# Softmax stage of a graph network: the destinations' one-hot made in 16 bits, two tiles innermost, and widened to fp32 by ScalarE

## The chip, the cores and the metric

The kernel runs on one core of a Trainium2 chip. The metric is the device time of one execution in microseconds; lower is better. A time of a kernel is the median of its runs.

## The reference, cut to what matters

Four graph layers run in a row on 3125 nodes with 16 features and 100000 edges sorted by destination. The change is in the second layer, an attention over the edges that end in one node:

```
w_m = (efeat @ W_msg + b_msg).reshape(E, 16, 16)
w_a = (efeat @ W_attn + b_attn).reshape(E, 16, 16)
h_src = feat[src][:, :, None]
e1 = w_m * h_src
e2 = w_a * h_src
seg_max = segment_max(e2, dst)
ex = exp(e2 - seg_max[dst])
denom = segment_sum(ex, dst)
ft = segment_sum(e1 * ex / denom[dst], dst)
out = ft.sum(axis=1)
```

The softmax stage, `soft_sums`, computes `ex` and `e1 * ex` of every edge (256 values each) and sums both by destination. The division by `denom` is left to the stage behind it, `attend`.

## The kernel before

**Tiles.** The edges lie in NT = 832 tiles of 128 slots, an edge to a partition. A block is 128 nodes (NB = 25 blocks), each tile has the edges of one block only, and two neighbouring tiles always share one. The number of a destination within its block is the field `LO` of `m.fields`, which is fp32; holes have -1 there.

**Rounds.** `soft_sums` goes through 416 rounds `r` of two tiles, written out without a loop. Two rounds make a group `n` of four tiles (HB = 4, 208 groups). One round does this:

- TensorE, `network`: four bf16 matmuls of 256 columns give `net_a` and `net_m` in PSUM (three sets of buffers).
- VectorE, `enter`: two operations multiply them by the source's features `m.held`.
- TensorE, `top`: six bf16 matmuls subtract the maxima of the block, which a second one-hot, `hot_t`, spreads over the edges. VectorE makes `hot_t` once per group in `far_hot`.
- ScalarE: `Exp` of `net_a` into `both[..., 0, :]`.
- VectorE, `weigh`: `both[..., 1, :] = net_m * both[..., 0, :]`.
- TensorE, `spread`: for each of the two tiles an fp32 matmul of 512 columns with the one-hot `hot` as weights, into `sums`. The profile has two rows for one such matmul.
- VectorE, `add`: adds `sums` to the row of the block in `m.acc`.

`hot` is the one-hot that this change is about: for each edge 128 fp32 values, 1.0 in the column of its destination. `spread_hot(n)` makes it for four tiles at once with `one_hot` (line 1271): `LO`, repeated over 128 columns, is compared with `m.iota_row`. Both inputs are fp32 in SBUF. It has two buffers, used in turn.

**Order.** Each engine's order is written out by hand. TensorE goes, for round r, `network(r + 3)`, `top(r + 2)`, `spread(r + 1)`. VectorE's order is:

```
for r in range(turns):
    if r % 2 == 0 and r + 2 < turns:
        far_hot(r // 2 + 1)
    if r + 2 < turns:
        enter(r + 2)
    if r + 1 < turns:
        weigh(r + 1)
    add(r)
    if r % 2 == 0 and r + 2 < turns:
        spread_hot(r // 2 + 1)
```

**GpSimd.** Beside this, GpSimd writes the edges' second records into DRAM in another order (`m.slots2`), for a later stage: 832 indirect DMAs, two to a round (line 1533), whose indices `row2` and data `rec2` lie in SBUF. No engine of this stage waits for them. To spread them over the stage, their first in a round waits until `add(r - 2)` is done (`kept`), the second until `weigh(r)` is done (`both_s`). After the last of them GpSimd waits for the landing of all. The stage is a block: `attend`, which begins on VectorE at line 1674, starts when all engines have left it.

**Start.** VectorE's first instruction in the stage is the clearing of `m.acc` (line 1577), then `far_hot(0)`, `spread_hot(0)`, `enter(0)`, `enter(1)`, `weigh(0)`.

Of the kernel before, what the change touches and what calls it, by code (L numbers as in the profile page):

```python
# [5 lines left out]
ALU = mybir.AluOpType  # L6
# [4 lines left out]
BF16 = mybir.dt.bfloat16  # L11
FP16 = mybir.dt.float16

P = 128
# [9 lines left out]
NT = -(-2 * ((E + NB * (2 * P - 1)) // (2 * P)) // (2 * TB)) * 2 * TB  # L24
# [7 lines left out]
WGT, SRC, TIX, LO, SRCC, KEY, LOE, NF = range(8)  # L32
# [24 lines left out]
def makers(nc, ctx, stage):  # L57

    def sb(name, shape, dt=F32):
        return ctx.enter_context(nc.sbuf_tensor(f"{stage}_{name}", shape, dt))  # L60

    def ps(name, shape, dt=F32):
        return ctx.enter_context(nc.psum_tensor(f"{stage}_{name}", shape, dt))

    def sem(name):
        made = nc.alloc_semaphore(f"{stage}_{name}")
        ctx.callback(PAST.append, made)
        return made

    return sb, ps, sem  # L70
# [738 lines left out]
def slot_field(m, t0, n, k):  # L809

    return m.fields[:, bass.ds(t0, n), k]


def blocks_of(nc, m, engine, pair, n):

    _, values = nc.values_load_multi_w_load_instructions(m.pair[0:1, bass.ds(pair, n)], engines=[engine], min_val=0, max_val=NB - 1,
                                                         skip_runtime_bounds_check_because=COUNTED)
    return values
# [412 lines left out]
HB = 4  # L1231
# [38 lines left out]
def one_hot(nc, m, field, n, out):  # L1270
    return nc.vector.tensor_tensor(out, slot_field(m, n * HB, HB, field)[:, :, None].to_broadcast([P, HB, P]),
                                   m.iota_row[:, None, :].to_broadcast([P, HB, P]), ALU.is_equal)
# [218 lines left out]
def soft_sums(nc, m):  # L1491

    turns, sets = NT // 2, 3
    with ExitStack() as ctx:
        sb, ps, sem = makers(nc, ctx, "sm")
        feat, low = sb("feat", [KP, 2, 512], BF16), sb("low", [P, 2, 512], FP16)
        hot_t, hot = sb("hot_t", [P, 2, 512], BF16), sb("hot", [P, 2, HB, P])
        both = sb("both", [P, 2, 2, 2, 256])
        rec2, row2 = sb("rec2", [P, NT, 2]), sb("row2", [P, NT], I32)
        net_a, net_m = ([ps(f"{n}{k}", [P, 2, 256]) for k in range(sets)] for n in ("net_a", "net_m"))  # L1500
        sums = [ps(f"sums{k}", [P, 512]) for k in range(2)]
        loaded = [sem("loaded0"), sem("loaded1")]
        names = ("hot_t_s", "hot_s", "net_s", "arg_s", "mess_s", "tops_s", "exp_s", "both_s", "sums_s", "kept", "cleared",
                 "ordered", "order_in")
        (hot_t_s, hot_s, net_s, arg_s, mess_s, tops_s, exp_s, both_s, sums_s, kept, cleared, ordered,
         order_in) = map(sem, names)
        block = ctx.enter_context(nc.Block())

        @block.sync
        def _(sp):  # L1510
            low_rows = m.low_row.rearrange("(c n) -> c n", n=512)
            feats = m.feat_t.rearrange("k (c n) -> k c n", n=512)
            for n in range(HT):
                h = n % 2
                if n >= 2:
                    sp.wait_ge(net_s, 2 * n - 2)
                    sp.wait_ge(hot_t_s, n - 1)
                sp.dma_start(low[:, h], low_rows[n:n + 1].to_broadcast([P, 512])).then_inc(loaded[h], 16)
                sp.dma_start(feat[:, h], feats[:, n, :]).then_inc(loaded[h], 16)
                if n == 1:  # L1520
                    sp.dma_start(rec2[:, :, :], m.rec2_dram).then_inc(order_in, 16)
                    sp.dma_start(row2[:, :], m.row2_dram).then_inc(order_in, 16)
# [14 lines left out]
        def four(ap):  # L1537
            return ap.rearrange("q t (i o) -> q t i o", o=D)

        @block.vector  # L1540
        def _(dve):
            def far_hot(n):
                h = n % 2
                dve.wait_ge(loaded[h], (n // 2 + 1) * 32)
                if n >= 2:
                    dve.wait_ge(tops_s, 2 * n - 2)
                nc.vector.tensor_scalar(hot_t[:, h], low[:, h], m.iota_col[:, 0:1], None, ALU.is_equal).then_inc(hot_t_s, 1)

            def spread_hot(n):
                if n >= 2:  # L1550
                    dve.wait_ge(sums_s, 2 * n - 2)
                one_hot(nc, m, LO, n, hot[:, n % 2]).then_inc(hot_s, 1)

            def enter(r):
                k = r % sets
                src = m.held[:, 2 * r:2 * r + 2, :][:, :, :, None].to_broadcast([P, 2, D, D])
                dve.wait_ge(net_s, r + 1)
                nc.vector.tensor_tensor(four(net_a[k][:, :, :]), four(net_a[k][:, :, :]), src, ALU.mult).then_inc(arg_s, 1)
                nc.vector.tensor_tensor(four(net_m[k][:, :, :]), four(net_m[k][:, :, :]), src, ALU.mult).then_inc(mess_s, 1)

            def weigh(r):
                dve.wait_ge(exp_s, r + 1)
                dve.wait_ge(mess_s, r + 1)
                nc.vector.tensor_tensor(both[:, r % 2, :, 1, :], net_m[r % sets][:, :, :], both[:, r % 2, :, 0, :], ALU.mult).then_inc(both_s, 1)  # L1564

            values = []

            def add(r):
                if r % 8 == 0:
                    values[:] = blocks_of(nc, m, mybir.EngineType.DVE, r, 8)  # L1570
                row = m.acc[:, bass.ds(values[r % 8], 1), :].rearrange("q o c -> q (o c)")
                dve.wait_ge(sums_s, r + 1)
                if r:
                    dve.wait_ge(kept, r)
                nc.vector.tensor_tensor(row, row, sums[r % 2][:, :], ALU.add).then_inc(kept, 1)

            nc.vector.memset(m.acc[:, :, :], 0.0).then_inc(cleared, 1)
            dve.wait_ge(cleared, 1)
            far_hot(0)
            spread_hot(0)  # L1580
            enter(0)
            enter(1)
            weigh(0)
# [11 lines that stand above are left out]
        @block.scalar  # L1595
        def _(act):
            for r in range(turns):
                act.wait_ge(tops_s, r + 1)
                if r >= 2:
                    act.wait_ge(sums_s, r - 1)  # L1600
                nc.scalar.activation(both[:, r % 2, :, 0, :], net_a[r % sets][:, :, :], ACT.Exp).then_inc(exp_s, 1)  # L1601

        @block.tensor
        def _(pe):
# [588 lines left out]
def build(nc, a, out):  # L2193
# [17 lines left out]
    with ExitStack() as ctx:  # L2211
# [44 lines left out]
        with ExitStack() as scope:  # L2256
            rb = on(scope)
            m.top3, m.held = rb("top3", [P, NB, 3, 256], BF16), rb("held", [P, NT, D])
            normalise(nc, m, "n1")
            attention_rows(nc, m)  # L2260
            with ExitStack() as tops:
                m.top = on(tops)("top", [P, NB, 256])
                segment_max(nc, m)
                split_top(nc, m)
            m.acc = rb("acc", [P, NB, 512])
            soft_sums(nc, m)
            attend(nc, m)
# [52 lines left out]
```

## Time and profile before

| what | value |
| --- | --- |
| median of three runs | 8238.34 us |
| the runs | 8241.7, 8238.34, 8218.16 us |
| the profiled execution, its own time | 8244.08 us |
| its span in the trace | 8242.4 us |
| softmax stage in the span | about 3998 to 5218 us |
| VectorE busy in the whole span | 72% |
| TensorE busy in the whole span | 70% |
| GpSimd busy in the whole span | 55% |
| ScalarE busy in the whole span | 20% |

Times in rows are microseconds from the start of the span. A row of a timeline gives start, length, engine, line, operation, output and inputs, the shape (partitions x elements per partition), the number of instructions merged, and in brackets how long the engine had been idle before it and what ended that. A row of groups gives the count, then the busy time in us and the mean of one in ns, then the idle time before them. PE is TensorE, PEld its weight load, DVE VectorE, ACT ScalarE, POOL GpSimd. The record of a VectorE instruction goes on a little after the next has started, so what one costs is the distance from its start to the next one's start.

### The profile page before, as it was taken

What the parts mean: (1) busy time and instruction counts of PE and PEld (TensorE: products, weight loads), DVE (VectorE), ACT (ScalarE), POOL (GpSimd) and SP (SyncE); (2) the same over time, 40 slices, a digit from 0 to 9 for tenths busy, and PEclk for the clock granted to TensorE, in tenths of its full rate; (3) what the DMA queues carried; (4) which work ended last, traced back from release to release, by engine and by line L of the source; (5) the groups of instructions that cost most, each with busy time, mean ns of one, the idle gap of its engine ahead of it and who ended that gap; (6) DMA issues with size and microseconds to landing.
All of it is one profiled execution on the core that took longest, in us unless ns stands there. A gap on an engine that the chain in (4) does not pass through costs nothing. (4 is left out here: it accounts for less than half of the span.)

```text
span 8242.4 us, 120531 instructions
## 1 busy us (share of the span) xinstructions
PE 5734.8 (70%) x33629; PEld 3891.4 (47%) x33630; DVE 5955.1 (72%) x11485; ACT 1609.0 (20%) x2672; POOL 4496.5 (55%) x4143
## 2 busy tenths in 40 slices
PE   3433333256444588887699999455479699999999
PEld 2333333146444455555455555144334366666555
DVE  5766555275333499998899999799600388888898
ACT  0010111101000255554122222044000022222000
POOL 0488888487777577777377777200000277777000
PEclk9999999855555699999899999699889655555899
DMA  2122222332111333334211111022263411112000
GB/s 99 41 60 57 56 55 58 77 83 53 37 37 36 49 84 85 83 85 79 42 44 43 44 43 44 15 109 110 80 264 136 151 32 32 32 32 32 1 0 1
DMA packets 486789, 514.88 MB, mean 62 GB/s; under 512 B 258365, under 2 KB 388805, under 8 KB 476106
## 3 DMA queue, kind: packets, MB, share of 16 engines
q1 hardware_dynamic: 343198, 446.64, 17.5%
q0 software_dynamic: 132160, 43.97, 6.7%
q10 hardware_dynamic: 11232, 21.73, 0.9%
q8 instruction: 111, 1.82, 0.1%
q14 instruction: 88, 0.72, 0.0%
HBM read 415.02 MB, written 95.99 MB: 62 GB/s over the span
## 5 line engine op out<-in xcount | busy, mean ns | idle before, releaser
L1284 POOL DMA_INDIRECT sh_ring<-node,sh_idx x832 | 858.6, 1032 | 1488.2 <-DVE sh_idx L1921 1229.4
L424 POOL DMA_INDIRECT slots<-rank_staged,rank_row_i x800 | 998.7, 1248 | 265.5 <-issue 260.0
L1533 POOL DMA_INDIRECT slots<-sm_rec,sm_row x832 | 900.0, 1082 | 388.0 <-issue 215.2
L1360 POOL DMA_INDIRECT mx_ring<-node,mx_idx x832 | 857.8, 1031 | 322.3 <-issue 248.5
L935 POOL DMA_INDIRECT mid_ring<-typed,mid_idx x832 | 875.8, 1053 | 259.2 <-issue 253.4
L404 PE MATMUL rank_found<-rank_next_sb,rank_hot_hi_t 25*125 25x128 f32 x1600 | 374.3, 422 | 764.0 <-ACT rank_next_sb L386 748.5
L1643 PE MATMUL sm_sums<-sm_both,sm_hot 128*128 128x512 f32 x1664 | 786.8, 595 | 0.4 <-DVE sm_both L1564 0.2
L404 PEld LDWEIGHTS rank_found<-rank_next_sb,rank_hot_hi_t 25*125 25x125 f32 x1600 | 347.4, 323 | 789.8 <-issue 734.9
L1140 PE MATMUL mid_sums<-mid_ring,mid_hot_d 128*128 128x17 f32 x1664 | 391.7, 375 | 459.3 <-DMA mid_ring<-typed,mid_idx 446.9
L1140 PEld LDWEIGHTS mid_sums<-mid_ring,mid_hot_d 128*128 128x128 f32 x1664 | 383.3, 312 | 476.0 <-issue 476.0
L2161 PE MATMUL srl_sums<-srl_outer,srl_hot_lo 128*128 128x400 f32 x1664 | 561.9, 501 | 7.4 <-DVE srl_outer L2143 7.4
L1383 DVE TENSOR_TENSOR_SCAN mx_run<-mx_far,mx_run,mx_logit 128x512 f32<-128x512 f32 x414 | 509.1, 1272 | 21.5
L695 PE MATMUL adj_sums<-adj_heavy,adj_hot 128*128 128x128 bf16 x4224 | 322.7, 222 | 244.0 <-DVE adj_heavy L644 129.1
L1464 PE MATMUL mx_best<-mx_run_e,mx_hot 128*128 128x256 f32 x1664 | 418.8, 395 | 50.7 <-ACT mx_run_e L1414 50.3
L2161 PEld LDWEIGHTS srl_sums<-srl_outer,srl_hot_lo 128*128 128x128 f32 x1664 | 317.4, 191 | 252.8 <-DVE srl_outer L2143 9.1
L2061 PE MATMUL sh_hid_ps<-sh_ends_t,mlp 32*128 32x512 f32 x416 | 392.8, 1096 | 56.8 <-ACT sh_ends_t L2014 56.8
L1601 ACT ACTIVATE sm_both<-sm_net_a 128x512 f32<-128x512 f32 x416 | 248.6, 598 | 938.1 <-PE sm_net_a L1630 933.7
L695 PEld LDWEIGHTS adj_sums<-adj_heavy,adj_hot 128*128 128x128 bf16 x4224 | 245.0, 98 | 323.2 <-issue 275.5
L1053 DVE COPY mid_ring<-fields 128x8 f32<-128x8 f32 x104 | 18.8, 181 | 505.0 <-PE mid_sums L1142 505.0
L1643 PEld LDWEIGHTS sm_sums<-sm_both,sm_hot 128*128 128x128 f32 x1664 | 283.2, 190 | 209.8 <-issue 200.7
L1707 DVE TENSOR_TENSOR agg<-c_sums,dinv_row 128x3200 f32<-128x3200 f32 x4 | 14.0, 3492 | 501.8 <-PEq L1746 501.8
L2068 PE MATMUL sh_v_ps<-mlp,sh_hid 128*128 128x32 f32 x1664 | 374.5, 401 | 0.0
(404 smaller groups left out, 12727.3 us busy)
## 6 DMA issues: line engine op xcount, KB each, us to landing
strips<-near SPq DMA_DIRECT2D x76, 1600.0 KB, 14.4
mx_far<-far_row SPq DMA_DIRECT2D x208, 256.0 KB
rank_key_row<-key_rows SPq DMA_DIRECT2D x100, 488.3 KB
near<-adj_whole SPq DMA_DIRECT2D x175, 256.0 KB, 2.0
sm_low<-low_row SPq DMA_DIRECT2D x208, 128.0 KB
sh_low<-low_row SPq DMA_DIRECT2D x104, 256.0 KB, 3.3
feat_t<-mid_out ACTq DMA_DIRECT2D x104, 204.0 KB
mx_feat<-feat_t SPq DMA_DIRECT2D x208, 102.0 KB
```

What stands on the lines that cost most here:

```text
L404: last = nc.tensor.matmul(found[h][:, j, :], hot_hi_t[:, h, j, :], next_sb[:, h, j * P:(j + 1) * P], start=True, stop=True, skip_group_che ...
L424: pool.indirect_dma_start(m.slots, bass.IndirectOffsetOnAxis(ap=row_i[:, h, j:j + 1], axis=0), staged[:, h, j, :], None).then_inc(sent[h], 16)
L695: last = nc.tensor.matmul(sums[:, bass.ds(at[j], P)], hot[:, h, j // 2, :, j % 2], heavy[:, h, k, j // 2, :, j % 2], start=False, stop=Tru ...
L935: pool.indirect_dma_start(ring[:, n % DEEP, j, 0:D], None, m.typed, bass.IndirectOffsetOnAxis(ap=idx[:, t:t + 1], axis=0)).then_inc(gather ...
L1140: nc.tensor.matmul(sums[:, bass.ds(blocks[j // 2] * K17, K17)], hot_d[:, h, j, :], ring[:, n % DEEP, j, 0:K17], start=False, stop=True, sk ...
L1284: pool.indirect_dma_start(ring[:, h, j, :], None, table, bass.IndirectOffsetOnAxis(ap=idx[:, h, j:j + 1], axis=0)).then_inc(part, 16)
L1360: pool.indirect_dma_start(ring[:, n % DEEP, j, :], None, m.node40, bass.IndirectOffsetOnAxis(ap=idx[:, t:t + 1], axis=0)).then_inc(gathere ...
L1383: last = nc.vector.tensor_tensor_scan(run[:, h, c, :], far[:, h, :], logit[:, c, :], before, ALU.add, ALU.max)
L1464: last = nc.tensor.matmul(best[:, k, :], hot[:, h, 2 * k + j, :], run_e[:, h, 2 * k + j, :], start=j == 0, stop=j == 1, skip_group_check=True)
L1533: pool.indirect_dma_start(m.slots2, bass.IndirectOffsetOnAxis(ap=row2[:, t:t + 1], axis=0), rec2[:, t, :], None).then_inc(ordered, 16)
L1643: last = nc.tensor.matmul(sums[r % 2][:, :], hot[:, h, 2 * (r % 2) + j, :], both[:, r % 2, j].rearrange("q a c -> q (a c)"), start=j == 0, ...
L2161: last = nc.tensor.matmul(sums[:, 0:NB * D], hot_lo[:, h, j, :], outer[:, h, j, :], start=False, stop=True, skip_group_check=True)
```

## The change

`spread_hot` compares in 16 bits. The stage first makes `lo16`, `LO` of all tiles as bf16, and `iota`, the numbers 0 to 127 as bf16, each twice side by side. The one-hot of a group then goes into `hot16`, bf16, in an order with two tiles innermost, `[pair of tiles, column, tile]`, so that the innermost run of both inputs and of the output is two neighbouring elements. Numbers up to 127 and -1 are exact in bf16. ScalarE then copies `hot16` into `hot`, which is fp32 in the old order, right behind the `Exp` of each even round. `hot16` has one buffer: VectorE waits for the copy of the group before. The wait for `hot`'s older readers (`sums_s`) moves from VectorE to ScalarE. TensorE's waits stay the same; `hot_s` now comes from ScalarE.

```diff
         hot_t, hot = sb("hot_t", [P, 2, 512], BF16), sb("hot", [P, 2, HB, P])
+        lo16, iota, hot16 = sb("lo16", [P, NT], BF16), sb("iota", [P, P, 2], BF16), sb("hot16", [P, HB // 2, P, 2], BF16)
...
+            pairs = [P, HB // 2, P, 2]
+
             def spread_hot(n):
-                if n >= 2:
-                    dve.wait_ge(sums_s, 2 * n - 2)
-                one_hot(nc, m, LO, n, hot[:, n % 2]).then_inc(hot_s, 1)
+                if n >= 1:
+                    dve.wait_ge(hot_s, n)
+                nc.vector.tensor_tensor(hot16[:, :, :, :], lo16[:, n * HB:(n + 1) * HB].rearrange("q (a t) -> q a t", t=2)[:, :, None, :].to_broadcast(pairs),
+                                        iota[:, None, :, :].to_broadcast(pairs), ALU.is_equal).then_inc(hot16_s, 1)
...
             nc.vector.memset(m.acc[:, :, :], 0.0).then_inc(cleared, 1)
-            dve.wait_ge(cleared, 1)
+            nc.vector.tensor_copy(lo16[:, :], m.fields[:, :, LO]).then_inc(cleared, 1)
+            nc.vector.tensor_copy(iota[:, :, :], m.iota_row[:, :, None].to_broadcast([P, P, 2])).then_inc(cleared, 1)
+            dve.wait_ge(cleared, 3)
             far_hot(0)
             spread_hot(0)
...
                 nc.scalar.activation(both[:, r % 2, :, 0, :], net_a[r % sets][:, :, :], ACT.Exp).then_inc(exp_s, 1)
+                if r % 2 == 0:
+                    n = r // 2
+                    act.wait_ge(hot16_s, n + 1)
+                    if n >= 2:
+                        act.wait_ge(sums_s, 2 * n - 2)
+                    nc.scalar.copy(hot[:, n % 2].rearrange("q (a t) c -> q a t c", t=2),
+                                   hot16[:, :, :, :].rearrange("q a c t -> q a t c")).then_inc(hot_s, 1)
```

VectorE at the start of the stage, before:

```order
L1577 MEMSET acc 128x12800
L1547 TENSOR_SCALAR sm_hot_t<-sm_low,iota_col 128x512
L1271 TENSOR_TENSOR sm_hot<-fields,iota_row 128x512
L1558 TENSOR_TENSOR sm_net_a<-sm_net_a,held 128x512
L1559 TENSOR_TENSOR sm_net_m<-sm_net_m,held 128x512
```

And with the change (`sm_lo` is `lo16`, `sm_iota` is `iota`, `sm_hot` stands for `hot16` as well as for `hot`):

```order
L1581 MEMSET acc 128x12800
L1582 CAST sm_lo<-fields 128x832
L1583 CAST sm_iota<-iota_row 128x256
L1548 TENSOR_SCALAR sm_hot_t<-sm_low,iota_col 128x512
L1555 TENSOR_TENSOR sm_hot<-sm_lo,sm_iota 128x512
L1562 TENSOR_TENSOR sm_net_a<-sm_net_a,held 128x512
L1563 TENSOR_TENSOR sm_net_m<-sm_net_m,held 128x512
```

Two casts have come in ahead of `far_hot(0)`; the rest stands as it did, and so does the order of VectorE in every later round, where line 1555 takes the place of line 1271.

ScalarE in the stage, one piece of the difference:

```order
-L1601 ACTIVATE sm_both<-sm_net_a 128x2x256 x416
+L1607 ACTIVATE sm_both<-sm_net_a 128x2x256
+L1613 CAST sm_hot<-sm_hot 128x512
+L1607 ACTIVATE sm_both<-sm_net_a 128x2x256 x2
+L1613 CAST sm_hot<-sm_hot 128x512
```

Where ScalarE had 416 `Exp` in a row, a copy of 512 elements per partition now stands behind every second one.

## Rows read from the trace of the kernel before

**Rows 1.** Windows, steady stage: length, busy of PE, PEld, DVE, ACT, POOL; clock, DMA

```profile
4020.00:5180.00 1160.00, 1160.00 (x5752) 678.65 (x5751) 1160.00 (x2054) 245.61 (x411) 871.03 (x804) 1.00 0.18 43
```

**Rows 2.** Timeline, VectorE, one group of four tiles in mid-stage

```profile
4302.20 0.68 DVE L1271 TENSOR_TENSOR sm_hot<-fields,iota_row 128x512 f32<-128x512 f32 x1
4302.80 0.69 DVE L1558 TENSOR_TENSOR sm_net_a<-sm_net_a,held 128x512 f32<-128x512 f32 x1
...
4305.19 0.34 DVE L1547 TENSOR_SCALAR sm_hot_t<-sm_low,iota_col 128x512 bf16<-128x512 f16 x1
...
4305.45 0.69 DVE L1558 TENSOR_TENSOR sm_net_a<-sm_net_a,held 128x512 f32<-128x512 f32 x1
...
4307.85 0.68 DVE L1271 TENSOR_TENSOR sm_hot<-fields,iota_row 128x512 f32<-128x512 f32 x1
```

**Rows 3.** Timeline, the same group: TensorE's spreads, the weigh ahead of one, ScalarE

```profile
4302.02 1.88 PE L1643 MATMUL sm_sums<-sm_both,sm_hot 128*128 128x512 f32 x4
...
4302.22 0.60 ACT L1601 ACTIVATE sm_both<-sm_net_a 128x512 f32<-128x512 f32 x1 [2.24 <-PE sm_net_a L1630]
...
4304.00 0.68 DVE L1564 TENSOR_TENSOR sm_both<-sm_net_m,sm_both 128x512 f32<-128x512 f32 x1
...
4304.83 1.90 PE L1643 MATMUL sm_sums<-sm_both,sm_hot 128*128 128x512 f32 x4
...
4307.67 1.88 PE L1643 MATMUL sm_sums<-sm_both,sm_hot 128*128 128x512 f32 x4
```

**Rows 4.** Timeline, GpSimd, the same group

```profile
4302.31 1.42 POOL L1533 DMA_INDIRECT slots<-sm_rec,sm_row  x1 [0.30 <-DVE acc L1575]
4304.03 0.97 POOL L1533 DMA_INDIRECT slots<-sm_rec,sm_row  x1 [0.30 <-issue]
4305.31 1.07 POOL L1533 DMA_INDIRECT slots<-sm_rec,sm_row  x1 [0.30 <-DVE acc L1575]
```

**Rows 5.** Timeline, early in the stage: GpSimd and VectorE

```profile
4064.75 0.97 POOL L1533 DMA_INDIRECT slots<-sm_rec,sm_row  x1 [0.41 <-DVE sm_both L1564]
...
4067.75 0.97 POOL L1533 DMA_INDIRECT slots<-sm_rec,sm_row  x1 [0.74 <-DVE sm_both L1564]
...
4064.99 0.69 DVE L1271 TENSOR_TENSOR sm_hot<-fields,iota_row 128x512 f32<-128x512 f32 x1
...
4066.79 0.68 DVE L1564 TENSOR_TENSOR sm_both<-sm_net_m,sm_both 128x512 f32<-128x512 f32 x1
```

**Rows 6.** Timeline, GpSimd: second and last of seven long stops

```profile
4340.51 0.97 POOL L1533 DMA_INDIRECT slots<-sm_rec,sm_row  x1 [4.62 <-issue]
...
5159.37 0.97 POOL L1533 DMA_INDIRECT slots<-sm_rec,sm_row  x1 [4.53 <-issue]
```

**Rows 7.** Timeline, the end of the stage and the start of the next

```profile
5186.53 0.69 DVE L1564 TENSOR_TENSOR sm_both<-sm_net_m,sm_both 128x512 f32<-128x512 f32 x1
...
5189.90 0.69 DVE L1575 TENSOR_TENSOR acc<-acc,sm_sums 128x512 f32 x1 [1.03 <-PE sm_sums L1643]
...
5212.11 0.97 POOL L1533 DMA_INDIRECT slots<-sm_rec,sm_row  x1 [0.30 <-issue]
5218.10 6.82 DVE L1674 TENSOR_SCALAR att_none<-acc 128x6400 f32<-128x6400 f32 x1 [27.51 <-PEq L1494]
```

**Rows 8.** Groups by line and form, VectorE, whole span: two one-hots of 1024

```profile
L1054 DVE TENSOR_TENSOR mid_hot_s<-mid_lo,iota_row 128x1024 bf16<-128x1024 bf16 x104 | 126.8, 1219 | 0.0
...
L641 DVE TENSOR_TENSOR adj_hot<-adj_now,adj_iota 128x1024 bf16<-128x1024 bf16 x176 | 120.5, 685 | 0.0
```

**Rows 9.** One line each, VectorE, two casts of other stages: min/median/max ns, start

```profile
L1389 DVE CAST mx_idx<-fields x1: 923/923/923, 2811.3 to 2811.3; 128x832 int32<-128x832 f32 x1
...
L615 DVE CAST adj_iota<-iota_row x1: 229/229/229, 5329.4 to 5329.4; 128x256 bf16<-128x256 f32 x1
```

**Rows 10.** Groups, ScalarE: copies from SBUF of 128 and of 512

```profile
L663 ACT COPY adj_sums<-adj_zeros 128x512 f32<-128x512 f32 x175 | 103.3, 590 | 6.9
...
L2027 ACT COPY parts<-sh_both 128x128 f32 x102 | 30.4, 298 | 105.8 <-DVE sh_three L1995 105.8
```

**Rows 11.** Groups, GpSimd, an early and a late window of the stage

```profile
L1533 POOL DMA_INDIRECT slots<-sm_rec,sm_row x103 | 100.0, 970 | 45.6 <-DVE sm_both L1564 30.1 <-issue 15.5
...
L1533 POOL DMA_INDIRECT slots<-sm_rec,sm_row x107 | 118.6, 1108 | 32.6 <-issue 32.6
```

More of the change, by code:

```diff
@@ L1503, in soft_sums @@
         names = ("hot_t_s", "hot_s", "net_s", "arg_s", "mess_s", "tops_s", "exp_s", "both_s", "sums_s", "kept", "cleared",
-                 "ordered", "order_in")
+                 "ordered", "order_in", "hot16_s")
         (hot_t_s, hot_s, net_s, arg_s, mess_s, tops_s, exp_s, both_s, sums_s, kept, cleared, ordered,
-         order_in) = map(sem, names)
+         order_in, hot16_s) = map(sem, names)
         block = ctx.enter_context(nc.Block())
```

## The prediction

> **What bounds the kernel now.** I read the windows of the stage first, then single rounds on each engine, then the stage's two ends. In the windows TensorE and VectorE are both busy 1160 of 1160 us, at a granted clock of 1.00, which is the 2.4 GHz level, and GpSimd 871 of 1160 [rows 1]. Two engines at 100% say that relief of one alone may give nothing, so the distances of starts must tell which of them holds the other.
>
> VectorE needs 5.65 us for a group of four tiles (two rounds): from the one-hot at 4302.20 to the next at 4307.85 [rows 2]. In this group the one-hot takes 0.60 us, start to start, `far_hot` 0.26, and eight others about 0.60 each (5.65 - 0.60 - 0.26 = 4.79 by eight). No gap is left. TensorE's spreads start at 4302.02, 4304.83 and 4307.67, so its rounds take 2.81 and 2.84 us [rows 3]. The spread of 4304.83 has a `weigh` that ended at 4304.68, 0.15 us before it; the round that starts there is the one of 2.84. I read it thus: TensorE sets the pace, and VectorE holds it by 0.02 to 0.03 us in every second round. Each is full to within half a per cent.
>
> The third engine is the one to watch. The last `add` ends at 5189.90 + 0.69 = 5190.59, but the next stage starts at 5218.10, and what ends last in between is GpSimd, whose last DMA starts at 5212.11 and ends at 5213.08 [rows 7]. **GpSimd is behind by some 24 us, and these lie bare on the path**: VectorE has been idle 27.51 us. How it got there: early in the stage its DMAs take 970 ns each and it waits for VectorE (45.6 us idle over 103 DMAs, 30.1 of them for `weigh`); late they take 1108 ns and it waits for no one, only 0.30 us of issue ahead of each [rows 11]. Seven times in the stage, once every 113 DMAs, it stops for 3.0 to 5.0 us (4.62 and 4.53 in the two shown, 0.30 would be usual) [rows 6], and afterwards it doesn't catch up. It can't, because of the one-hot: a DMA that starts at 4302.31, when the one-hot has run since 4302.20, takes 1.42 us and not 0.97, and one that starts at 4305.31, 0.12 after `far_hot`, takes 1.07 [rows 2, 4]. So the stalls are 0.45 and 0.10 us a group. Undisturbed, four DMAs would take 4 x (0.97 + 0.305) = 5.10 us; with the stalls they take 5.65, just VectorE's pace. The two engines run in step: if GpSimd is early, it meets more of the one-hot and is held longer. A lag once gained stays.
>
> The Trainium skill has this as a rule (SBUF — State Buffer, "Who interferes with whom"): a VectorE instruction with two SBUF inputs contends with a GpSimd instruction that reads SBUF. The 1.42 us agree with it; `enter`, `weigh` and `add` have an input in PSUM and lengthen no DMA here.
>
> **The change part by part.**
>
> *The one-hot on VectorE.* Only the form counts. At 1024 elements the form with one element repeated takes 1219 ns even in bf16, and the form with pairs innermost, which the adjacency stage has already, 685 ns: 534 less for 1024, so 267 less for 512 [rows 8]. 0.60 - 0.27 = 0.33 us, start to start. 208 times 0.27 is 55 us less on VectorE, and nearly all of it turns into idle time, since TensorE is full.
>
> *Steady pace.* VectorE's group falls to 5.38 us, TensorE's stays. What TensorE gets back is its 0.02 us in every second round: 208 x 0.02 = **-4 us**. Bounds: 0, if the 2.84 is TensorE's own; -13, if its rounds had a floor of 2.79 (four rows of 0.427 and ten bf16 matmuls of 0.108 by their start distances in this group), 0.03 under the mean of 2.82, 416 times. I take -4, since the 2.81 rounds show no wait.
>
> *The copy on ScalarE.* No row shows this form. From SBUF, 128 elements take 298 ns and 512 (into PSUM) 590 [rows 10]; I take 0.60, with 0.50 and 1.20 as bounds (twice, for the input with a stride). ScalarE is idle 2.24 us before each `Exp` [rows 3]. The place: `Exp` runs 4302.22 to 4302.82, the one-hot will be there at about 4302.6, the copy ends at about 4303.5, and its reader is the spread at 4304.83. 1.3 us are left, 0.7 at the upper bound. Cost 0. If that cover were gone, TensorE would wait.
>
> *VectorE's new wait* for the copy of the group before: that copy ended over 4 us earlier. Cost 0. Behind it on VectorE stand `enter` and `weigh`, for which TensorE waits.
>
> *GpSimd.* A DMA is held from its start to about 0.56 us after the start of the one-hot (4302.31 + 0.45 - 4302.20) [rows 2, 4]. The new one streams 0.27 us less, so it can hold one DMA for 0.29 at most. With `far_hot` (0.10 as seen, 0.2 as a bound) a group costs GpSimd at most 5.10 + 0.29 + 0.20 = 5.59 us, under TensorE's 5.63. So it can't be held in step any more, and gains between 0.04 and 0.53 us on each group, mostly over 0.3, since few starts fall into so short a window. A stop of 4.3 us extra is made up in some 10 to 14 groups, and there are 28 groups from one to the next. From the last one at 5159.37, 41 DMAs are left, 10 groups: I leave 0.7 us of lag (0 to 2). Without lag a DMA starts 0.28 us after the `weigh` it waits for ends (4066.79 + 0.68 to 4067.75) [rows 5]. The last `weigh` ends at 5187.22, but the DMA ahead of it takes its time as well; I put the last one's end at 5189.0. That and the 5.02 us from its end to the next stage, which I keep, give 5194.0, plus 0.7, against 5218.10: **-23.4 us**. VectorE's own end, 5190.59, is before that.
>
> *Start.* Two casts stand ahead of `far_hot(0)`: 923 and 229 ns by the nearest rows [rows 9], some 0.1 less each by start distance, plus 0.1 for the wait: 1.1 us. `enter(0)` comes 0.27 earlier by the shorter one-hot. **+0.9 us** (0.5 to 2).
>
> Sum: 0.9 - 4 - 23.4 = **-26.5 us**. The profiled execution took 8244.08 us, which gives 8217.6. The median shown is 5.7 lower, so the forecast for it is 8238.3 - 26.5 = **8211.8 us**. The three runs differ by 23.5 us; whether the one at 8218 had no lag on GpSimd I can't see. That is the weak point of setting the sum against the median. A measurement can tell about 0.3%, 24.7 us, from no change; the forecast is just over that.
>
> **The rivals.**
>
> 1. *GpSimd stays in step* (no gain at the end). The hold might not shrink with the streaming time, or another pair of collisions might add up to 0.5 us. For: the lock held through four different phases before. Against: `far_hot`, which streams shorter (0.26 us start to start), holds shorter (0.10). Then only 0.9 - 4 = -3 is left: 8235. Chance 0.13.
> 2. *The 16-bit form isn't faster here*, VectorE stays at 0.60, and all stays but the start: 8239. Against: line 641 has the same pattern and shows it. Chance 0.04.
> 3. *Slower*: GpSimd holds VectorE. A one-hot that starts while a DMA runs would have to wait for it, up to 0.97 us. VectorE has 0.25 us a group to spare now, so this decides from a wait of 0.25 on, and costs 208 times what is over it: up to 208 x 0.72 = 150 us, so about 8365; a wait of 0.5 would give 52 - 3 = +49, with the lag on top, so about 8290. Against: the one-hot at 4064.99 started in the midst of the DMA of 4064.75 and took 0.69 like all [rows 5]. The other slow way, a copy of over 1.9 us, has no row near it. Chance 0.03. The Trainium skill (SBUF — State Buffer, "SBUF: two separate sides") says of this pair of ports that whoever starts first has it for the whole instruction and the other fully blocks. By this rule the time would be the one of this rival; the row at 4064.99 doesn't bear it out for VectorE, while the DMA of 1.42 us does for GpSimd.
> 4. *More*: TensorE's floor is 2.79, and the steady pace gives -13. 8238.3 + 0.9 - 13 - 23.4 = 8203. Chance 0.08.
>
> The forecast itself has 0.72, split by the threshold (8213.6): a lag of 2 us left or a start of +2 brings it under 0.3%. I give 0.44 above it and 0.28 within.
>
> **The numbers.** Faster: 0.44 + 0.08 = 0.52. Same: 0.28 + 0.13 + 0.04 = 0.45. Slower: 0.03. The forecast's own range is 8205 to 8217 by the bounds. The median's share of runs like the 8218 one can take some 10 us more off, so the low end is 8196; the high end reaches to rival 1, 8236.
>
> **What would show it.** In the profile after: line 1555 at about 0.42 us and 0.33 to the next start; VectorE with gaps of some 0.25 us a group, TensorE still full, rounds of 2.81; ScalarE's copy at 0.6 us, over 1 us ahead of the spread; GpSimd's DMAs back to 0.97 to 1.0 on average, with waits for `weigh` and `kept` up to the end, and the last one before 5192; `attend` some 5 us behind it. Wrong it would be if GpSimd's DMAs still took 1.1 us late in the stage, if TensorE waited for `hot_s`, or if line 1555 took 0.68.

## The result

The changed kernel takes **8196.41 us** (median of 11 runs, 8187.43 to 8219.95), the one before, measured on the same chip in turn, 8226.29 us (11 runs, 8218.16 to 8241.7). The ratio is 0.9963, with an interval of 0.9953 to 0.9973: 22 to 39 us faster. Repeated on another chip it is 0.9957 (0.9939 to 0.9974), 8189.27 against 8221.59 us. The time lies just inside the forecast's range and 15 us under the forecast of 8211.8, of which 12 are the median of before: 8226.29 and not 8238.34. Every kernel further down had one run, unless a number of runs or an interval stands beside it.

### The profile after

The same windows as [rows 1], with the same columns:

```profile
4020.00:5150.00 1130.00, 1130.00 (x5623) 664.33 (x5622) 1116.09 (x2009) 341.55 (x603) 777.73 (x803) 1.00 0.19 44
```

TensorE is still busy throughout at a granted clock of 1.00, VectorE 1116 of 1130 us. A row of VectorE lasts some 0.09 us into the next, so its real slack is more than these 14 us: by start distances it is about 0.2 us a group. The timeline of one group, all four engines, against [rows 2 to 4]:

```profile
4301.48 0.97 POOL L1534 DMA_INDIRECT slots<-sm_rec,sm_row  x1 [0.50 <-DVE sm_both L1568]
...
4301.87 0.42 DVE L1555 TENSOR_TENSOR sm_hot<-sm_lo,sm_iota 128x512 bf16<-128x512 bf16 x1
...
4302.05 1.88 PE L1656 MATMUL sm_sums<-sm_both,sm_hot 128*128 128x512 f32 x4
4302.21 0.69 DVE L1562 TENSOR_TENSOR sm_net_a<-sm_net_a,held 128x512 f32<-128x512 f32 x1
4302.25 0.60 ACT L1607 ACTIVATE sm_both<-sm_net_a 128x512 f32<-128x512 f32 x1 [2.22 <-PE sm_net_a L1643]
...
4302.75 0.61 ACT L1613 CAST sm_hot<-sm_hot 128x512 f32<-128x512 bf16 x1
4302.75 0.96 POOL L1534 DMA_INDIRECT slots<-sm_rec,sm_row  x1 [0.30 <-issue]
...
4304.36 0.97 POOL L1534 DMA_INDIRECT slots<-sm_rec,sm_row  x1 [0.65 <-DVE sm_both L1568]
...
4304.69 0.35 DVE L1548 TENSOR_SCALAR sm_hot_t<-sm_low,iota_col 128x512 bf16<-128x512 f16 x1
...
4304.87 1.88 PE L1656 MATMUL sm_sums<-sm_both,sm_hot 128*128 128x512 f32 x4
...
4307.50 0.42 DVE L1555 TENSOR_TENSOR sm_hot<-sm_lo,sm_iota 128x512 bf16<-128x512 bf16 x1
```

The one-hot costs 0.34 us, start to start (4301.87 to 4302.21), where it cost 0.60. The copy on ScalarE follows `Exp`, takes 0.61 and ends 1.5 us before the spread that reads it (4303.36 to 4304.87). A group takes 5.63 us (4301.87 to 4307.50), and not 5.65. GpSimd's DMAs take 0.97 us and wait for `weigh` (`sm_both`) in mid-stage, where in [rows 4] one took 1.42 and another 1.07. Over the whole stage, the page's groups for these DMAs and for those of another stage:

```profile
L424 POOL DMA_INDIRECT slots<-rank_staged,rank_row_i x800 | 981.9, 1227 | 265.8 <-issue 257.9
L1534 POOL DMA_INDIRECT slots<-sm_rec,sm_row x832 | 809.8, 973 | 446.5 <-DVE sm_both L1568 201.2
```

The mean is 973 ns. Before it was 970 early and 1108 late [rows 11]; now GpSimd waits 201.2 us for `weigh` over the stage. The long stops are still there, the last of them this one, of the length of [rows 6]:

```profile
5110.48 0.97 POOL L1534 DMA_INDIRECT slots<-sm_rec,sm_row  x1 [4.51 <-issue]
```

The end of the stage, against [rows 7]:

```profile
5162.56 0.96 POOL L1534 DMA_INDIRECT slots<-sm_rec,sm_row  x1 [0.30 <-issue]
...
5163.83 0.69 DVE L1579 TENSOR_TENSOR acc<-acc,sm_sums 128x512 f32 x1 [1.03 <-PE sm_sums L1656]
5168.54 6.82 DVE L1687 TENSOR_SCALAR att_none<-acc 128x6400 f32<-128x6400 f32 x1 [4.02 <-PEq L1494]
```

The last DMA ends (5163.52) before the last `add` starts (5163.83), and `attend` follows that start by 4.71 us instead of 28.20. The start of the stage:

```profile
3976.29 0.33 SPq L1519 DMA_DIRECT2D sm_low<-low_row  x1
...
3989.68 0.76 DVE L1582 CAST sm_lo<-fields 128x832 bf16<-128x832 f32 x1
3990.36 0.28 DVE L1583 CAST sm_iota<-iota_row 128x256 bf16<-128x256 f32 x1
...
3990.94 0.42 DVE L1555 TENSOR_TENSOR sm_hot<-sm_lo,sm_iota 128x512 bf16<-128x512 bf16 x1
3991.28 0.69 DVE L1562 TENSOR_TENSOR sm_net_a<-sm_net_a,held 128x512 f32<-128x512 f32 x1
```

From SyncE's first issue (3976.29) to the first `enter` (3991.28) it is 14.99 us, against 14.37 before. From now on each kernel's stage is given in the same three parts, from the same rows of its timeline; "us a group" is twice the mean distance of two `Exp` starts over 340 rounds. What follows rests on these parts and not on the time of a single run: the runs above scatter by some 30 us, while the stage of a second profile of either kernel came out within 2.2 us of the first (1221.78 and 1192.87, further down).

| kernel | first issue to `enter` | `enter` to last `add` | last `add` to `attend` | stage | us a group | mean DMA, ns |
|---|---|---|---|---|---|---|
| before | 14.37 | 1177.06 | 28.20 | 1219.63 | 5.648 | 1082 |
| after | 14.99 | 1172.55 | 4.71 | 1192.25 | 5.629 | 973 |
| difference | +0.62 | -4.51 | -23.49 | -27.38 | | |

The two profiled executions differ by more, 8244.08 - 8194.21 = 49.9 us. Nearly all the rest is in stages that the change doesn't touch: the ranking loop with line 424 took 1270.5 us and now 1254.0 (its DMAs 1248 and 1227 ns on average, with the same code), two others 3.9 and 2.7 us less. These vary from one execution to the next.

### The profile page after: what moved, and what is told of

Its sections match the earlier page's. It is cut to its first block and busy times, and to the rows that moved or that the text cites. A ratio compares the mean times of both kernels' runs of the same rounds, so it can differ in the third digit from the quotient of the medians.

```text
span 8192.5 us, 120947 instructions
## 1 busy us (share of the span) xinstructions
PE 5729.7 (70%) x33629; PEld 3892.4 (48%) x33630; DVE 5945.6 (73%) x11487; ACT 1713.4 (21%) x2880; POOL 4383.3 (54%) x4143
## 5 line engine op out<-in xcount | busy, mean ns | idle before, releaser
L424 POOL DMA_INDIRECT slots<-rank_staged,rank_row_i x800 | 981.9, 1227 | 265.8 <-issue 257.9
L1534 POOL DMA_INDIRECT slots<-sm_rec,sm_row x832 | 809.8, 973 | 446.5 <-DVE sm_both L1568 201.2
```

What stands on the lines that cost most here:

```text
L424: pool.indirect_dma_start(m.slots, bass.IndirectOffsetOnAxis(ap=row_i[:, h, j:j + 1], axis=0), staged[:, h, j, :], None).then_inc(sent[h], 16)
L1534: pool.indirect_dma_start(m.slots2, bass.IndirectOffsetOnAxis(ap=row2[:, t:t + 1], axis=0), rec2[:, t, :], None).then_inc(ordered, 16)
```

## The experiments

**My theory**: the 24 us at the end came from GpSimd being held in step with VectorE by the long one-hot; the shorter one can't hold it. "Held" is a DMA whose row is longer than its usual 0.97 us while a VectorE instruction runs; "in step" is a GpSimd whose holds repeat group by group and keep it at VectorE's pace. **Rivals**: GpSimd was late merely because it waits for `kept` and `both_s` ("late by its waits"), or what counted was that VectorE had no slack. The label's first letter says whether a kernel starts from before (b) or after (a). Kernels under one heading ran on one chip.

### Four kernels on a chip of another kind

`b_eight_dmas` does only the first eight of the 832 DMAs:

```
-            for r in range(turns):
...
+            for t in range(8):
+                pool.indirect_dma_start(...).then_inc(ordered, 16)
+            pool.wait_ge(ordered, 16 * 8)
```

> The kernel before with 8 of GpSimd's 832 indirect DMAs in the softmax stage (the second records of the other tiles are not written). The stage, from its first DMA issue to attend's first instruction, took 1219.6 us before and 1192.3 us after. In step (my theory: GpSimd is held by the one-hot and can't make up its stops, and this lag lies bare at the end): the pace of a group stays at 5.65 us, the 28.2 us from the last add to attend fall to about 4.7, the stage is 1196 us. Pace (rival: what counts is how much work VectorE has, and GpSimd also slows it): the group itself gets shorter than 5.64, and the stage is under 1192.

`b_free_dmas` drops GpSimd's waits: `pool.wait_ge(kept, r - 1)` and `pool.wait_ge(both_s, r + 1)` are gone.

> The kernel before, with GpSimd's DMAs waiting for nothing but their own data. Late by its waits (rival: GpSimd is late because each DMA waits for add or weigh): 832 x 1.275 us and seven stops of 4.3 more are about 1091 us, so it is done some 90 us ahead of VectorE, the stage is 1196 us. In step (my theory): soon after the start it meets the one-hots and is held at VectorE's pace, 208 x 5.65 us, and every stop adds to that, so about 1175 + 30 us from its first DMA: the stage is 1210 to 1220 us, and its DMAs take about 1.1 us on average.

`a_one_element` keeps the copy on ScalarE, but makes the 16-bit one-hot in the form with one element repeated, `lo16[...][:, :, None].to_broadcast([P, HB, P])` against an `iota` of `[P, P]`.

> The kernel after with one element, not a pair, innermost: lo16, iota and hot16 stay bf16, the copy by ScalarE stays, all waits stay, the one-hot should take 0.68 us again. In step: VectorE's group is 5.65 us, the hold is 0.45 us again and the lag of GpSimd grows to 20 to 28 us; stage about 1220 us. If moving the fp32 one-hot to ScalarE (the widening and its waits) were what gained, the stage would stay at 1192 to 1197 us.

`a_pad_two_inputs` puts an operation with two SBUF inputs ahead of each one-hot, so that the pair streams about as long as the old one-hot did:

```
+                    nc.vector.tensor_tensor(extra[...], m.fields[:, 0:16, :], m.fields[:, 16:32, :], ALU.add)
                 nc.vector.tensor_tensor(hot16[...], ...)
```

> The kernel after, with one more VectorE operation right ahead of each new one-hot: 112 elements, two fp32 inputs in SBUF, result unused (0.18 us start to start by estimate, 0.12 of it streaming). VectorE's group is then about 5.56 us, still under TensorE's 5.63. In step: both together can hold a DMA for up to 0.29 + 0.18 = 0.47 us, and 0.43 beside far_hot's 0.10 is enough to hold GpSimd at TensorE's pace; the lag comes back, the stage is 1205 to 1220 us. Pace: VectorE still has room, so nothing changes, 1192 us.

They took 9126.0, 10190.91, 9340.58 and 9336.85 us, beside 9347.63 for the kernel before: this chip needs 1100 us more for it than those of the result. Where GpSimd issues DMAs, the other engines go slower there, at 6.62 us a group in `a_one_element` (stage 1399.5). So its time says nothing on the question, and neither does that of `a_pad_two_inputs` (1399.2). Two things can still be read. With eight DMAs the stage of before takes 1192.97 us, `enter` to last `add` 1177.39, as with all of them on the chip of the result (1177.06), and `attend` follows the last `add` by 1.02 us instead of 28.20. So there the DMAs cost the steady pace nothing, and all of their price is at the end. And with nothing to hold it back GpSimd issues all 832 while the rest nearly stands still (`b_free_dmas`, windows with the DMAs and after them; columns as in [rows 1]):

```profile
4620.00:5740.00 1120.00, 178.89 (x445) 76.64 (x442) 95.95 (x154) 17.92 (x30) 820.75 (x818) 0.53 0.03 4
5800.00:6860.00 1060.00, 1058.53 (x5240) 618.51 (x5238) 1057.65 (x1873) 223.72 (x375) 0.00 (x0) 1.00 0.15 42
```

### The next three, again on such a chip

`a_pad_one_input` is the control of the padded one: `nc.vector.tensor_reduce(extra, m.fields[:, 0:16, :], ...)`, as many elements from one input.

> The kernel after, with one more VectorE operation right ahead of each new one-hot: the sum of the same 112 elements, with one input in SBUF (0.18 us start to start by estimate). It costs VectorE what the run with two inputs costs, but should hold no DMA. In step: no lag, stage 1192 us. Pace: the same as the run with two inputs, whatever that is.

`a_eight_dmas` is the changed kernel with eight DMAs.

> The kernel after with 8 of GpSimd's 832 indirect DMAs in the softmax stage (the second records of the other tiles are not written). In step: GpSimd's lag is gone in the kernel after, so nothing is left to gain: stage 1192 us, group 5.63 us, and 4 us less than the same cut of the kernel before. If GpSimd still cost something, the stage would be shorter by that.

`a_clear_on_pool` moves the clearing of `m.acc` off VectorE:

```
+            pool.memset(m.acc[:, :, :], 0.0).then_inc(acc_s, 1)
             pool.wait_ge(order_in, 32)
...
-            nc.vector.memset(m.acc[:, :, :], 0.0).then_inc(cleared, 1)
```

> The kernel after, with the clearing of acc (10.7 us on VectorE at the start of the stage, while TensorE waits 9 us for enter) moved to GpSimd, and add(0) waiting for it. Every theory: VectorE starts its rounds up to 10 us earlier, if GpSimd clears as fast as VectorE; add(0) then waits for GpSimd some us. In step says that GpSimd's late start does no harm, since it can make up for a lag in the kernel after: stage 1183 to 1188 us, ratio to before about 0.995 to 0.996. Were GpSimd unable to catch up, its 10 us would show at the end and the stage stay at 1192 us. If GpSimd clears at half VectorE's rate (20 us), add(0) waits and nothing is gained, or up to 4 us lost.

Before took 9327.38 here (14 runs). `a_pad_one_input` took 9343.87 and tells nothing. `a_eight_dmas` took 9108.43; its stage is 1190.07 us, against 1192.97 for `b_eight_dmas`. So with eight DMAs the whole change is worth 2.9 us: 5.629 against 5.646 us a group, less the 0.4 of the start. **The gain at the end needs the DMAs.** `a_clear_on_pool` took 9299.2 (9 runs), a ratio to before of 0.9965 (0.9951 to 0.9978).

### Both kernels once more

> The kernel before, unchanged, for its trace on the chip of this call. Four runs of the first call took 9337 to 9348 us with the kernel before at 9347.63, where the kernel before had taken 8218 to 8242 us: engines wait for issue and for nothing the profile shows while GpSimd's DMAs run. If this is a matter of the chip, this run is either near 8240 with a stage of 1219 us and a bare end of 28 us, or near 9340 with a stage of about 1400 us.

> The kernel after, unchanged, on the same chip. In step: on a chip like the first the stage is 1192 us and the ratio to before 0.9963. On a chip like those of the last two calls the stage is not bound by TensorE or VectorE but by the waits for issue, VectorE's 55 us are then hidden as well, and the ratio is 0.998 to 1.000.

This chip is of the first kind (before 8221.59). `b_again` took 8244.85 in its one run, with a stage of 1221.78; `a_again` 8189.27 (9 runs), with 1192.87. GpSimd's groups of `b_again`, early and late in the stage:

```profile
L1533 POOL DMA_INDIRECT slots<-sm_rec,sm_row x99 | 106.9, 1080 | 35.1 <-issue 18.2 <-DVE acc L1575 12.2 <-DVE sm_both L1564 4.6
...
L1533 POOL DMA_INDIRECT slots<-sm_rec,sm_row x90 | 99.6, 1107 | 32.0 <-issue 32.0
```

and the same windows (4160 to 4300 and 5000 to 5130 us) of `a_again`:

```profile
L1534 POOL DMA_INDIRECT slots<-sm_rec,sm_row x99 | 95.9, 969 | 42.3 <-DVE sm_both L1568 25.8 <-issue 16.5
...
L1534 POOL DMA_INDIRECT slots<-sm_rec,sm_row x93 | 90.0, 968 | 41.0 <-DVE sm_both L1568 21.6 <-issue 19.1 <-DVE acc L1579 0.3
```

How long after the end of the `add` that it depends on a DMA starts grows in `b_again` from 1.0 us to 3.0, 7.4, 11.3, 15.7, 20.0, 24.3 and 28, a step at each of the seven stops. In `a_again` it is back at 0.8 to 0.9 within 5 to 9 groups of each.

### The four that had told nothing, on a chip of the first kind

`b_free_2` and `a_one_2` are `b_free_dmas` and `a_one_element`, `a_pad_two_2` and `a_pad_one_2` the padded ones.

> The kernel before, with GpSimd's DMAs waiting for nothing but their own data, on another chip than the last time. Late by its waits: done some 90 us ahead of VectorE, the stage is 1196 us. In step: held at VectorE's pace soon after the start, each of its seven stops adding up, its DMAs 1.1 us on average, stage 1210 to 1220 us. If the chip is like the second one, the stage is near 2260 us again and tells neither.

> The kernel after with one element, not a pair, innermost: still bf16, still widened by ScalarE, the one-hot 0.68 us. In step: VectorE's group is 5.65 us, the hold is 0.45 us again, GpSimd's lag grows to 20 to 28 us, stage about 1220 us. If it were the move to ScalarE that gained, 1192 to 1197 us.

> The kernel after, with one more VectorE operation right ahead of each new one-hot: 112 elements, two fp32 inputs in SBUF. In step: VectorE's group of 5.56 us still fits under TensorE's 5.63, but both together can hold a DMA for 0.47 us, the lag comes back, stage 1205 to 1220 us. Pace: nothing changes, 1192 us.

> The kernel after, with one more VectorE operation right ahead of each new one-hot: the sum of the same 112 elements, one input in SBUF. In step: it costs VectorE as much but holds no DMA, no lag, stage 1192 us. Pace: the same as the run with two inputs.

| kernel | us | to `enter` | to last `add` | to `attend` | stage | us a group | mean DMA, ns |
|---|---|---|---|---|---|---|---|
| before, this chip | 8224.57 | | | | | | |
| `b_free_2` | 8209.11 | 14.51 | 1176.68 | 19.27 | 1210.47 | 5.647 | 1101 |
| `a_one_2` | 8223.19 | 15.19 | 1176.64 | 29.43 | 1221.26 | 5.647 | 1088 |
| `a_pad_two_2` | 8197.8 | 14.99 | 1174.37 | 4.88 | 1194.23 | 5.629 | 978 |
| `a_pad_one_2` | 8187.57 | 14.99 | 1172.95 | 4.89 | 1192.83 | 5.629 | 978 |

**`b_free_2` shows the step plainly.** GpSimd's timeline in mid-stage, with no wait left in its loop:

```profile
4297.40 1.42 POOL L1529 DMA_INDIRECT slots<-sm_rec,sm_row  x1 [0.30 <-issue]
4299.13 0.97 POOL L1529 DMA_INDIRECT slots<-sm_rec,sm_row  x1 [0.31 <-issue]
4300.40 1.07 POOL L1529 DMA_INDIRECT slots<-sm_rec,sm_row  x1 [0.30 <-issue]
4301.77 0.97 POOL L1529 DMA_INDIRECT slots<-sm_rec,sm_row  x1 [0.30 <-issue]
4303.05 1.42 POOL L1529 DMA_INDIRECT slots<-sm_rec,sm_row  x1 [0.30 <-issue]
```

Four DMAs take 5.65 us (4297.40 to 4303.05), exactly VectorE's group, with the 1.42 and the 1.07 of [rows 4], though nothing in the program ties the two engines together. Its DMAs are held from the stage's start on, while it is some 8 us ahead of where the waits would have kept it. Free, it only wins these 8 us, and is 14 us late at the end. "Late by its waits" is refuted.

**`a_one_2` undoes the gain** with ScalarE's copy still in place. It is the form of the one-hot that matters, not its 16 bits and not where the fp32 comes from.

**`a_pad_two_2` missed.** Two short operations in a row don't hold like one long one. VectorE's and GpSimd's rows of one group:

```profile
4303.97 0.97 POOL L1535 DMA_INDIRECT slots<-sm_rec,sm_row  x1 [0.41 <-DVE sm_both L1571]
...
4304.27 0.27 DVE L1556 TENSOR_TENSOR sm_extra<-fields 128x112 bf16<-128x112 f32 x1
4304.45 0.42 DVE L1558 TENSOR_TENSOR sm_hot<-sm_lo,sm_iota 128x512 bf16<-128x512 bf16 x1
...
4305.24 0.96 POOL L1535 DMA_INDIRECT slots<-sm_rec,sm_row  x1 [0.30 <-issue]
```

After the first, no DMA of this kernel's stage takes over 1.15 us. But VectorE still had slack here, too (5.629 us a group), so the miss leaves open which of the two breaks the step. `a_pad_one_2` came as forecast (1192.83), but it is no control without a hold: 27 of its DMAs took 1.01 to 1.22 us.

### Hold and slack apart

`a_vector_full` is the one-input control with 28 tiles' fields in place of 16: VectorE has no slack, the hold stays short. `b_half_enter` keeps the old, long one-hot and gives VectorE slack: the second operation of `enter` works on `net_m[:, 0:1]` alone. `a_clear_2` is `a_clear_on_pool`.

> The kernel after, with a sum of 196 elements (one input in SBUF, result unused) right ahead of each new one-hot: by the 0.18 us that 112 elements cost, start to start, it costs 0.27 us. VectorE's group is then 5.65 us, what it was before the change, but the longest operation with two SBUF inputs stays the 16-bit one. In step: 5.65 - 5.10 = 0.55 us of hold would be needed, and 0.29 + 0.20 are to be had, so GpSimd makes up its stops: the end from the last add to attend stays at 4.7 to 6 us, only the pace is lost again, stage 1196 us. Pace: with VectorE's time of before the lag of before comes back, 1215 to 1220 us.

> The kernel before, in which enter multiplies only the first of the round's two tiles of net_m (the messages of the second tile are left without the source's factor): 0.53 us less per group on VectorE, twice what the change takes away, while the fp32 one-hot stays. In step: TensorE holds the pace at 5.63 us, GpSimd is still held for 0.45 + 0.10 us, the lag of 20 to 28 us stays bare at the end, stage 1212 to 1218 us. Pace: with VectorE well under TensorE the lag goes, stage 1192 us.

> The kernel after, with the clearing of acc moved from VectorE to GpSimd, on a chip where TensorE holds the pace. On the second kind of chip enter came 2.75 us earlier in the stage than in the kernel after (12.24 against 14.99 us from the first DMA issue), since GpSimd's clearing takes longer than VectorE's. In step: GpSimd's late start does no harm, so those 2 to 3 us are what is gained: stage 1189 to 1190 us. Were GpSimd unable to catch up, they would show at the end instead. The ratio to before should be 0.996, not to be told from the kernel after.

| kernel | us | to `enter` | to last `add` | to `attend` | stage | us a group | mean DMA, ns |
|---|---|---|---|---|---|---|---|
| before, this chip (17 runs) | 8222.74 | | | | | | |
| `a_vector_full` | 8204.89 | 14.99 | 1177.40 | 4.88 | 1197.27 | 5.646 | 1019 |
| `b_half_enter` | 8192.27 | 14.38 | 1174.08 | 4.72 | 1193.18 | 5.629 | 974 |
| `a_clear_2` | 8195.24 | 12.25 | 1174.01 | 4.72 | 1190.97 | 5.629 | 969 |

**`b_half_enter` missed, and taught most.** The long one-hot is there, and GpSimd isn't late. One group of it:

```profile
4301.82 0.96 POOL L1533 DMA_INDIRECT slots<-sm_rec,sm_row  x1 [0.30 <-DVE sm_both L1564]
4302.41 0.68 DVE L1271 TENSOR_TENSOR sm_hot<-fields,iota_row 128x512 f32<-128x512 f32 x1
4303.02 0.69 DVE L1558 TENSOR_TENSOR sm_net_a<-sm_net_a,held 128x512 f32<-128x512 f32 x1
4303.09 0.97 POOL L1533 DMA_INDIRECT slots<-sm_rec,sm_row  x1 [0.30 <-issue]
...
4304.90 0.97 POOL L1533 DMA_INDIRECT slots<-sm_rec,sm_row  x1 [0.85 <-DVE sm_both L1564]
4305.23 0.35 DVE L1547 TENSOR_SCALAR sm_hot_t<-sm_low,iota_col 128x512 bf16<-128x512 f16 x1
```

The DMAs start on either side of the one-hot and of `far_hot`. After a stop GpSimd is late, meets the one-hot and is held (up to 1.32 us), but comes free two rounds later:

```profile
4324.93 0.68 DVE L1271 TENSOR_TENSOR sm_hot<-fields,iota_row 128x512 f32<-128x512 f32 x1
4325.19 1.27 POOL L1533 DMA_INDIRECT slots<-sm_rec,sm_row  x1 [0.31 <-DVE acc L1575]
...
4327.74 0.35 DVE L1547 TENSOR_SCALAR sm_hot_t<-sm_low,iota_col 128x512 bf16<-128x512 f16 x1
...
4328.03 0.97 POOL L1533 DMA_INDIRECT slots<-sm_rec,sm_row  x1 [0.30 <-DVE acc L1575]
...
4330.56 0.74 DVE L1271 TENSOR_TENSOR sm_hot<-fields,iota_row 128x512 f32<-128x512 f32 x1
4330.58 0.97 POOL L1533 DMA_INDIRECT slots<-sm_rec,sm_row  x1 [0.30 <-issue]
```

**`a_vector_full`**: the pace of before is back and 4.9 us with it, the 23 us at the end are not. From the first stop to 4391 us GpSimd was in step nevertheless, with the operation that I had added as the second half of the hold:

```profile
4204.88 0.35 DVE L1556 TENSOR_REDUCE sm_extra<-fields 128x1 f32<-128x196 f32 x1
4205.00 1.41 POOL L1535 DMA_INDIRECT slots<-sm_rec,sm_row  x1 [0.30 <-DVE acc L1581]
4205.15 0.41 DVE L1557 TENSOR_TENSOR sm_hot<-sm_lo,sm_iota 128x512 bf16<-128x512 bf16 x1
...
4396.91 1.06 POOL L1535 DMA_INDIRECT slots<-sm_rec,sm_row  x1 [0.30 <-issue]
```

A one-input reduction lengthens a DMA, too, and here the two joined. The last row broke the step: that DMA started 0.12 us after the reduction (4396.79), as the one of 4205.00 did, and yet took 1.06 us and not 1.41; why is open. So this kernel, made to have a short hold, had a long one at times. Late in the stage it had broken free (the windows 4160 to 4300 and 5000 to 5130):

```profile
L1535 POOL DMA_INDIRECT slots<-sm_rec,sm_row x99 | 107.9, 1090 | 33.6 <-issue 18.3 <-DVE acc L1581 13.7 <-DVE sm_both L1570 1.6
...
L1535 POOL DMA_INDIRECT slots<-sm_rec,sm_row x91 | 88.8, 976 | 41.8 <-DVE sm_both L1570 24.8 <-issue 17.0
```

So in these two runs neither the long one-hot alone nor the full VectorE alone keeps GpSimd late to the end; both together do (before, `b_again`, `b_free_2`, `a_one_2`), and the change takes away both.

Why both are needed, the rows tell in part. To be kept at VectorE's 5.65 us a group, GpSimd must lose 5.65 - 5.10 = 0.55, and the one-hot gives about 0.45; the other 0.10 come from `far_hot`. A DMA let go by the one-hot puts the third start of the group 3.11 us after the one-hot's (4302.31 to 4305.31, plus the 0.11 by which it followed it). In the kernels that stay in step `far_hot` starts 2.99 us after the one-hot, 0.12 ahead of that DMA, which takes 1.07 [rows 2, 4]. In `b_half_enter` and after it starts 2.82 after it (4302.41 to 4305.23, 4301.87 to 4304.69). In the second fence of `b_half_enter` the third start is again 3.10 after the one-hot (4324.93 to 4328.03), but 0.29 after `far_hot`, and the DMA takes 0.97: `far_hot` is missed, and the next group's first DMA comes 0.02 after the one-hot (4330.58) instead of 0.11. There it isn't held. So it was all 14 times that a DMA of this kernel started within 0.03 us of the one-hot. But three DMAs of `b_free_2` that started as close behind it were held (1.49 to 1.52 us), so what decides there is open. A kernel that moves `far_hot` alone would test the rest; it wasn't run.

**`a_clear_2`** took 8195.24 us (12 runs; 0.9969, 0.9958 to 0.998): faster than before, and not to be told from the changed kernel. Its stage is the shortest of those with all DMAs, by 1.3 us. The memset on GpSimd holds VectorE's cast beside it; both, in the timeline:

```profile
4002.27 10.76 POOL L1527 MEMSET acc<- 128x12800 f32 x1 [69.77 <-POOLq L1475]
...
4002.31 11.36 DVE L1584 CAST sm_lo<-fields 128x832 bf16<-128x832 f32 x1 [0.32 <-PEq L1475]
```

The cast takes 11.36 us, and 0.76 where the memset isn't beside it. Only 2.74 us of the 10.7 that the clearing took on VectorE are won.

## Why the prediction was wrong

Each term of its sum came out near its size; **the base that the sum was set against was wrong**, and the reason given for GpSimd's term was half right. Step by step:

- *One-hot*: 0.60 to 0.33 us forecast, 0.60 to 0.34 measured. Nearly all of the 54 us (208 times 0.26) did turn into slack: TensorE stays full, and the pace falls by 4.5 us.
- *Steady pace*: -4 forecast, -4.5 measured. TensorE's rounds now take 2814.7 ns each, and before 2814 and 2833 in turn. Rival 4, a floor of 2.79, is out.
- *Copy on ScalarE*: 0.60 us forecast and 0.61 measured, 1.3 us of cover forecast and 1.5 measured. It costs nothing, nor does VectorE's new wait.
- *Start*: +0.9 forecast (its own terms give 1.1 - 0.27 = 0.83), +0.62 measured. The casts take 0.68 and 0.31 us by start distance, where I had 1.1 with the wait; the shorter one-hot gives 0.26 back.
- *GpSimd*: -23.4 forecast, -23.49 measured. The reason was half right. It was in step, as `b_free_2` shows, and the lag of each stop is now made up, in 5 to 9 groups where I had 10 to 14. But I argued from the length of the hold alone, by which `b_half_enter` would have stayed late; it ended in 1193.18 us, so slack on VectorE alone was enough, too. The number came out because it rests on the waits for `weigh`, not on the reason; that it did so to 0.1 us is luck, since the 0.7 us of lag that I had allowed for was not there (the lag of the last stop was made up in 8 groups of the 10).
- *Sum*: -26.5 forecast, -27.4 in the profiles, and 29.9 between the medians (22 to 39). Rival 1 (-3) and rival 2 are outside of that.
- *The base*, the step that failed: "The median shown is 5.7 lower, so the forecast for it is 8238.3 - 26.5". The median of before over 11 runs is 8226.29, 12.05 lower. By the same sum the forecast would have been 8199.8, 3.4 from the time. The three runs that I had are among the 11: they are the two longest and the shortest, so that their middle one lay high by the luck of the draw. I named the scatter of 23.5 us as the weak point, put it into the low end only, and left the likeliest time at the median of three. "8205 to 8217 by the bounds" isn't what the bounds give, either: +0.5 to +2, 0 to -13 and -24.1 to -22.1 on 8238.3 are 8202 to 8218. I had also wondered whether the run at 8218 lacked GpSimd's lag. The profiles speak against it: three executions in step end alike to within 1.3 us (28.20, 29.50 and 29.43 from the last `add` to `attend`), while the ranking stage alone differed by 16.5 us between two. None of them is that run, so this isn't shown.
- *Rival 3*, that GpSimd would hold VectorE: no one-hot waited for the rest of an indirect DMA, in any run. In the profile after, 195 of 208 start while one runs. The most that any was lengthened is 0.07 us (0.75 and not 0.68), 14 times in `b_half_enter`, with a DMA that started within 0.03 us of it; twice in after (0.45 and 0.46, not 0.42). The Trainium skill (SBUF — State Buffer, "SBUF: two separate sides") says that whoever starts first has the pair of ports for the whole instruction. The 11.36 us of the cast beside the memset agree with it; for an indirect DMA on GpSimd it doesn't hold here.

## What to carry to other kernels

Two engines that share nothing in the program can still run in step, when one holds the other in every turn of its loop, and then an engine with a tenth of its time to spare (5.10 of 5.65 us) never makes up a delay. The sign is an operation that is longer at a fixed phase of the other engine's loop, at a pace that matches that loop to the hundredth; either shortening the hold or giving the engine that holds slack may break it, so take the cheaper. And when a forecast is a difference of 0.3% of the time, three runs with a spread of 0.3% are no base for it: allow for the middle of the distribution lying elsewhere, on both sides.

## What the hardware showed beyond that

- **Two kinds of chip.** On two of the chips used the same kernel took 9347.63 and 9327.38 us, on the others 8221.59 to 8226.29. The extra time is in stages where GpSimd issues DMAs: three others take some 300 us more each, the ranking loop with its 800 of them none, and this one 178 (`a_one_element`: 1399.5 against the 1221.3 of `a_one_2`), but with eight DMAs this stage is as short as anywhere (1192.97). The engines then wait for "remote" and "issue", for nothing that the program names. Two large waits of the whole `a_one_element` (us in total, times, longest us); on the other chips no such wait stands there:

```profile
ACT mid_out L950 <- remote: 804.5, 50, 35.2
...
DVE mid_ring L1053 <- remote: 608.5, 29, 23.6
```

  What they wait for no run showed. With the clearing moved as well, the changed kernel was 0.9965 of before there; the change alone wasn't timed in several runs. What it gained there isn't the end of the stage: in `a_one_element` `attend` follows the last `add` by 4.88 us already.
- **One long stop for every 113 indirect DMAs**, of 3 to 5 us (2.96 to 5.05) where 0.30 is usual, in every kernel with all its DMAs and on both kinds of chip, always after the 113th, 226th, 339th and so on. It is harmless as long as GpSimd can catch up.
- **The first DMA of the stage** took 4.99 us in the profile after and 6.03 in `a_again`, and in both its row ends within 0.05 us of where the first `enter` starts (3986.33 + 4.99 = 3991.32, and 3991.28). In that of before it took 1.00. It isn't on the path, since the second one waits for `weigh` in any case; the cause is open.
